# Fused Flamingo layer pair on one core: 7 of 32 low parts of the attention probabilities moved to VectorE, the casts of five batches' rows moved to ScalarE, three buffers of fp32 probabilities

## The reference, cut to what matters

```
def _L0_xattn_ref(X, encoder_output, causal_mask, padding_mask, Wq, bq, Wk, bk, Wv, bv, Wo, bo):
    ...
    scores = jnp.einsum('bgrqd,bgkd->bgrqk', q, k) / jnp.sqrt(jnp.float32(HD))
    scores = jnp.where(causal_mask[None, None, None, :, :], -jnp.inf, scores)
    scores = jnp.where(padding_mask[:, None, None, None, :], -jnp.inf, scores)
    w = jax.nn.softmax(scores, axis=-1)
    out = jnp.einsum('bgrqk,bgkd->bgrqd', w, v)
    out = out.reshape(b, H, LQ, HD).transpose(0, 2, 1, 3).reshape(b, LQ, HID)
    return out @ Wo.T + bo
x = x + jnp.tanh(g_xattn[0]) * _L0_xattn_ref(_layernorm(x, axis=-1), ctx_2048, mask_SxS2_bc0, mask_BxS2_bk0, ...)
```

## Time and profile before

| what | value |
|---|---|
| median of three executions | 1724.37 us (1722.57 to 1724.7) |
| span of the profiled execution | 1722.0 us |
| mean granted TensorE clock | 0.978 |
| phase A's 256 steps | 77 to 504 us of the span |
| busy over the whole span | PE 92%, DVE 57%, POOL 48%, ACT 41% |

### The profile page before, as it was taken

How to read it: one execution, slowest core, us unless ns; L and a number is a source line. 1 busy time by engine, 2 the same in 40 slices (tenths; PEclk the granted TensorE clock), 3 DMA queues, 4 the chain that set the end, 5 groups by cost and what they waited for, 6 DMA issues and landing times. The chain is left out here.

```text
span 1722.0 us, 29300 instructions
## 1 busy us (share of the span) xinstructions
PE 1587.8 (92%) x10826; PEld 829.3 (48%) x10826; DVE 973.1 (57%) x1947; ACT 709.2 (41%) x1311; POOL 824.3 (48%) x853
## 2 busy tenths in 40 slices
PE   5769999999877999899999989999999999999998
PEld 3336665665443444345656544444444444444443
DVE  5736666778736999845665543377454333211146
ACT  3268888888855655532232321211111111222221
POOL 3478887877853545443452434344333532112134
PEclk9989999999878999999999999999999999999999
DMA  6745444322333555444554426447454754477746
GB/s 182 160 102 112 99 106 109 93 67 72 92 73 84 110 119 114 93 86 86 96 120 95 78 74 156 110 105 153 92 101 101 154 101 95 109 173 172 168 138 195
DMA packets 453955, 195.68 MB, mean 114 GB/s; under 512 B 395500, under 2 KB 418286, under 8 KB 453816
## 3 DMA queue, kind: packets, MB, share of 16 engines
q1 hardware_dynamic: 448136, 175.19, 46.0%
q0 software_dynamic: 5680, 18.62, 4.1%
HBM read 77.17 MB, written 22.81 MB: 58 GB/s over the span
## 5 line engine op out<-in xcount | busy, mean ns | idle before, releaser
L1109 POOL TENSOR_TENSOR a_pl<-a_prob,a_ph 128x512 f16<-128x512 f32 x256 | 295.2, 1166 | 72.7 <-ACT a_prob L996 72.3
L1199 DVE TENSOR_REDUCE a_mx<-bank 128x2 f32<-128x512 f32 x256 | 173.3, 686 | 97.1 <-PE bank L690 95.5
L140 PE MATMUL bank<-XTh,d_whs 128*128 128x512 f16 x512 | 194.9, 381 | 4.2 <-PEq L89 2.4
L141 PE MATMUL bank<-XTl,d_whs 128*128 128x512 f16 x512 | 194.7, 380 | 0.0
L142 PE MATMUL bank<-XTh,d_wls 128*128 128x512 f16 x512 | 194.6, 380 | 0.0
L995 ACT ACTIVATE a_ph<-bank 128x512 f16<-128x512 f32 x256 | 153.9, 601 | 73.3 <-PE bank L710 35.9
L2384 POOL CAST d_cut<-d_raw 128x512 f16<-128x512 f32 x90 | 56.2, 624 | 227.7 <-DMA d_raw<-in_L_ffn_sw 146.8
L996 ACT ACTIVATE a_prob<-bank 128x512 f32<-128x512 f32 x256 | 154.4, 603 | 0.0
L2304 DVE TENSOR_TENSOR d_hid<-d_hid,bank 128x512 f32<-128x512 f32 x64 | 43.9, 686 | 172.1 <-PE bank L142 168.2
L2295 ACT ACTIVATE d_hid<-bank 128x512 f32<-128x512 f32 x64 | 38.2, 597 | 204.7 <-PE bank L142 204.7
L2299 ACT ACTIVATE d_hh<-d_hid 128x512 f16<-128x512 f32 x64 | 40.3, 630 | 194.7 <-DVE d_hid L2304 194.7
(11 more groups left out here) (349 smaller groups left out, 3996.4 us busy)
## 6 DMA issues: line engine op xcount, KB each, us to landing
d_raw<-in_L_ffn_w SPq DMA_DIRECT2D x48, 256.0 KB, 3.1
d_raw<-in_L_ffn_sw SPq DMA_DIRECT2D x42, 256.0 KB, 3.1
made<-e_y SPq DMA_DIRECT2D x39, 256.0 KB
a_stage<-in_L_ffn_w_fc SPq DMA_DIRECT2D x32, 256.0 KB, 2.9
a_stage<-in_L_ffn_w_proj SPq DMA_DIRECT2D x32, 256.0 KB, 3.1
a_fbuf<-in_ctx SPq DMA_DIRECT2D x16, 256.0 KB, 3.5
rows<-f_cut SPq DMA_DIRECT2D x16, 256.0 KB, 2.5
out_x<-X SPq DMA_DIRECT2D x16, 256.0 KB, 2.4
```

Of the source, the lines that this page charges most:

```text
L140: nc.tensor.matmul(out_ap, lhi, rhi, start=first, stop=False)
L141: nc.tensor.matmul(out_ap, lhi, rlo, start=False, stop=False)
L1109: nc.gpsimd.tensor_tensor(pl[:, n % NP, :], prob[:, n % 2, :], ph[:, n % NP, :], ALU.subtract).then_inc(ev["L"], 1)
L1199: nc.vector.tensor_reduce(mx[:, h, tt, half, 2 * (g % 4):2 * (g % 4) + 2], bank[BS + m % 2][:, :].rearrange("p (r k) -> p r k", r=2), AX_X ...
```

## The change

Three things are changed in phase A.

1. The low parts of steps n = 3, 8, 12, 15, 20, 22 and 27 of every batch (`BY_DVE`) are made by VectorE, in `low_part`, two steps later in its order: at the head of steps 5, 10, 14, 17, 22, 24 and 29. GpSimd skips them. There are two counters now, `L` and `LD`, and `low_done` chooses which one is waited for.
2. The casts of batches 3 to 7's context and x rows are made by ScalarE, at the end of steps 4 and 7 (context) and 15 and 18 (x), with the waits that went with them: for the load of the rows, for the earlier transposes, and for the writes of the context's parts to HBM. GpSimd keeps the subtractions, in steps 6, 9, 17 and 20.
3. `a_prob` has three buffers, and exponential n waits for low part n-3 in place of n-2.

```
-    NP = 4
-    prob = sb("a_prob", [P, 2, D])
+    NP, NR = 4, 3
+    prob = sb("a_prob", [P, NR, D])
...
+    BY_DVE = (3, 8, 12, 15, 20, 22, 27)
+
+    def low_done(eng, m):
+
+        b, n = m // NS, m % NS
+        if n in BY_DVE:
+            eng.wait_ge(ev["LD"], len(BY_DVE) * b + BY_DVE.index(n) + 1)
+        else:
+            eng.wait_ge(ev["L"], (NS - len(BY_DVE)) * b + n + 1 - sum(i < n for i in BY_DVE))
...
-                wait("L", b, n + 3, NS)
+                low_done(pe, b * NS + n)
...
+            def ctx_high(f, t):
+                act.wait_ge(c_in[t], 16 * f + 16)
+                act.wait_ge(x_tp[(f - 1) % 2], xt_count(f - 1))
+                nc.scalar.activation(fcut[:, t, 0, :], fbuf[:, t, :], ACT.Copy).then_inc(c_hi, 1)
+
+            def x_high(f, t):
+                act.wait_ge(n_nrm, 2 * f + t + 1)
+                act.wait_ge(c_tp[f % 2], ct_count(f))
+                act.wait_ge(c_wr, 64 * (f + 1))
+                nc.scalar.activation(fcut[:, t, 0, :], fbuf[:, t, :], ACT.Copy).then_inc(x_hi, 1)
...
-                    wait("L", b, n + 1, NS)
+                    if b * NS + n >= NR:
+                        low_done(act, b * NS + n - NR)
                     nc.scalar.activation(ph[:, n % NP, :], bank[BST + n % 2][:, :], ACT.Exp)
-                    nc.scalar.activation(prob[:, n % 2, :], bank[BST + n % 2][:, :], ACT.Exp).then_inc(ev["E"], 1)
+                    nc.scalar.activation(prob[:, (b * NS + n) % NR, :], bank[BST + n % 2][:, :], ACT.Exp).then_inc(ev["E"], 1)
...
+                    if b + 3 < B and n in (4, 7):
+                        ctx_high(b + 3, (n - 4) // 3)
...
+                    if b + 3 < B and n in (15, 18):
+                        x_high(b + 3, (n - 15) // 3)
...
-            FRONT = {2: (ctx_high, 0), 4: (ctx_low, 0), 7: (ctx_high, 1), 9: (ctx_low, 1),
-                     14: (x_high, 0), 16: (x_low, 0), 19: (x_high, 1), 21: (x_low, 1)}
+            FRONT = {6: (ctx_low, 0), 9: (ctx_low, 1), 17: (x_low, 0), 20: (x_low, 1)}
...
-                    pool.wait_ge(ev["E"], b * NS + n + 3)
...
+                    if n not in BY_DVE:
+                        pool.wait_ge(ev["E"], b * NS + n + 3)
...
+            def low_part(b, n):
+                wait("E", b, n + 3, NS)
+                nc.vector.tensor_tensor(pl[:, n % NP, :], prob[:, (b * NS + n) % NR, :], ph[:, n % NP, :],
+                                        ALU.subtract).then_inc(ev["LD"], 1)
...
                 for n in range(NS):
+                    if n - 2 in BY_DVE:
+                        low_part(b, n - 2)
```

More of the change, by code:

```diff
@@ L383, in phase_a @@
              "lk0", "lk1", "hv0", "hv1", "lv0", "lv1", "tq", "tq0", "tq1", "tk", "cq", "ck", "S", "M", "nm",
-             "nt", "nc", "ng0", "ng1", "ST", "E", "L", "AV", "ON", "To0", "To1", "hO0", "hO1", "lO0", "lO1", "O0", "O1", "x0", "x1", "ch")
+             "nt", "nc", "ng0", "ng1", "ST", "E", "L", "LD", "AV", "ON", "To0", "To1", "hO0", "hO1", "lO0", "lO1", "O0", "O1", "x0", "x1", "ch")
     ev = {n: sem("a_" + n) for n in names}
@@ L1024, in _ @@
         def _(pool):
-            pool.sem_inc(ev["L"], 2)
             nc.gpsimd.memset(mhalf[:, :], -0.5).then_inc(n_half, 1)
@@ L1101, in _ @@
                 x_low(2, t)
-            FRONT = {2: (ctx_high, 0), 4: (ctx_low, 0), 7: (ctx_high, 1), 9: (ctx_low, 1),
-                     14: (x_high, 0), 16: (x_low, 0), 19: (x_high, 1), 21: (x_low, 1)}
+            FRONT = {6: (ctx_low, 0), 9: (ctx_low, 1), 17: (x_low, 0), 20: (x_low, 1)}
             def body(b, par, more, more2):
                 for n in range(NS):
-                    pool.wait_ge(ev["E"], b * NS + n + 3)
-                    nc.gpsimd.tensor_tensor(pl[:, n % NP, :], prob[:, n % 2, :], ph[:, n % NP, :],
-                                            ALU.subtract).then_inc(ev["L"], 1)
+                    if n not in BY_DVE:
+                        pool.wait_ge(ev["E"], b * NS + n + 3)
+                        nc.gpsimd.tensor_tensor(pl[:, n % NP, :], prob[:, (b * NS + n) % NR, :], ph[:, n % NP, :],
+                                                ALU.subtract).then_inc(ev["L"], 1)
                     g, k = front_at(b, n)
```

## The result

The changed kernel takes 1733.84 us in the median of 5 runs (1730.85 to 1737.51), against 1724.37 before (1722.40 to 1727.35 with the runs beside it). The ratio is 1.0050, 95% interval 1.0037 to 1.0063: slower by 0.5%. The forecast was 1726.7, the range 1715 to 1736. The profiled execution of the changed kernel is the slowest of the five, 1737.51 us with a span of 1735.8: 3.7 above its median, and 13.8 us longer in span than that of before. So the two profiles lie 4.3 us further apart than the medians.

The account below looks back on a forecast made before the run. TensorE was taken to bound batches 1 to 5, nobody being full in 0, 6 and 7. Terms +7.3 (batches 1 to 5), -3.0, 0 and -2.0 gave +2.3 on 1724.4: 1726.7 us, range 1715 to 1736.

Parts of the forecast that it names:

- The frame: Batches 1 to 5: TensorE is in front, so a faster GpSimd gives almost nothing and any TensorE wait is paid in full.
- the rival in which the blocking decides: VectorE's subtractions always lose to GpSimd's at step 3, overrun at 8, 12, 15, delay batch 6: some 1736; chance 0.15.
- Step 3: `times_v(3)` waits for VectorE's low part, half a lost race with GpSimd counted: +1.1 us a batch in batches 1 to 4, +4.4.
- Step 20: `times_v(20)` waits for VectorE's low part behind v's: +1.1 us in batches 1 to 3, half in 4 and 5; +4.4.
- Steps 8, 12, 15: VectorE's low parts there fit into 1.77 us of room even when blocked, by 0.2; costed at nothing.
- Exponentials: TensorE's wait for exponentials, 0.3 us in batch 2, can go, 5 times: -1.5 us.
- Batch 0: Cast on ScalarE directly before exponential 5, -1.2 us, and quicker catching up behind the stall, -1.8: -3.0, ends 0 and -7.
- Batch 6: VectorE rises to 48.0 of 50.60 us and replaces GpSimd as the bound: 0, ends -3 and +5.
- Batch 7: No maxima, VectorE has room, ScalarE has 5.4 us idle and TensorE is not full: -2.0 us, ends 0 and -4.
- ScalarE's waits for GpSimd below 5 us: Sign that the forecast is right: ScalarE's waits for GpSimd in phase A, 34.2 us for low parts before, fall below 5.
- that the relief wins: Rival: with fewer GpSimd operations all runs earlier and batches 0, 6 and 7 gain: -10 us, 1714; chance 0.25.
- A late ScalarE: Rival: the context-write waits and the casts moved to ScalarE reach the exponentials: +6 us on top, 1733; chance 0.07.

Follow-up runs that it names:

- casts and buffers: The changed kernel with no low part on VectorE; casts on ScalarE and three buffers stay: 1719.76 us, ratio 0.9972 to the kernel before.
- the version without steps 3 and 20: The changed kernel with the low parts of steps 3 and 20 on GpSimd again, five of 32 on VectorE: 1714.7 us, ratio 0.9949.
- a remade one: The kernel with short low parts, where VectorE also computes step 3's low part once more beforehand into a spare tile: 1739.32 us, ratio 1.0072.
- the kernel with short low parts: The changed kernel with GpSimd's low parts of steps 5, 9, 13 and 23 cut to 16 of 512 columns: 1723.81 us, ratio 0.9996.
- three buffers alone: The kernel before with only the third buffer of fp32 probabilities: 1723.32 us, ratio 0.9986.
- the low parts alone: The changed kernel with the casts back on GpSimd; seven low parts on VectorE and three buffers stay: 1739.14 us, ratio 1.0088.
- the kernel before with the earlier load: The kernel before, with SyncE's load of batch 3's context rows issued ahead of the output weight's eight transposes: 1717.23 us, ratio 0.9963.
- the version one step earlier: The changed kernel with all seven VectorE low parts made at the head of step n+1 rather than n+2: 1721.96 us, ratio 0.9994.

## Why the prediction came out as it did

Slower was the likeliest of the three verdicts, and the time is within the stated range of 1715 to 1736. The frame held too: in batches 1 to 5 TensorE is in front, and there a relieved GpSimd gives little (3.0 us for casts and buffers, 257.6 us against 260.6). But the sum itself was off: +2.3 forecast, +9.5 measured in the medians and +13.8 between the profiles. 1733.8 lies just outside the forecast's own range of 1721 to 1733, and the range held it thanks to the rival in which the blocking decides. That the verdict came out is in part luck, for the sum's own 1726.7 lies below the 1727.8 from which slower was counted. Step by step, against the profile:

- **Step 3, forecast +1.1 a batch in batches 1 to 4: right as a net, and by luck.** I had counted half a lost race. VectorE lost it in all four, for which the forecast had 1.7. But a blocked low part costs 1.50 us, not 1.85, since GpSimd starts 0.2 us earlier; the pause is 1.80. Against that stands the wait of 0.7 for a maximum, which is gone. Net 1.1: two errors that cancel. The casts give that 0.7 also without any low part on VectorE: against the version without steps 3 and 20 the full 1.80 is lost.
- **Step 20, forecast +4.4: 3.5** (three times 0.94, twice 0.33). The place and the cause, v's low part directly in front, are as told.
- **Steps 8, 12, 15 at nothing: right.** In batch 2 those of steps 8 and 12 were blocked and took 1.52 and 1.53 us, and step 8's left 0.34; that of step 15 was free (0.68). TensorE waited for none of them in batches 1 to 5.
- **Exponentials -1.5: right in kind**; batch 2 has no such wait left.
- **The term that was missing: TensorE's clock.** Four stretches at half clock in batches 1 to 4, 6.8 us. I priced a pause at its own length. This is the step that failed: with 7.3 forecast and 15.4 measured for batches 1 to 5, 6.8 of the 8.1 missing are this. The idle time of TensorE there grew by 8.2, near the forecast: 10.9 of waits for VectorE's low parts and 1.8 for the turned maxima's transfer at the end of batch 1, less 4.7 of waits for maxima, exponentials and an output's low part that are gone. Several of the variants have the transfer's wait at that place, and what sets it stays open. The kernels with a short pause (no stretch) and with a remade one (two) show that stretches come with the pause of step 3; in the changed kernel two of the four did, 3.4 us, and the other two stood behind other waits.
- **What the clock is in the medians stays open.** The whole program's granted clock was 0.978 in the profile before, near the top of the 67 timed executions of that kernel (0.967 to 0.979, mean 0.973), and 0.972 in the profile of the change, at the bottom of its five (0.972 to 0.976, mean 0.974). So the two profiles differ more in their clock than the kernels do on average, and how much of the 7.2 us by which the median exceeds the forecast is the clock's isn't shown. What the timed executions do show is the same direction in the kernel with short low parts: 0.977 in the mean of twelve, where the changed kernel has 0.974.
- **Batch 0, forecast -3.0: measured -3.0**, again as a sum of two: TensorE's stall fell from 12.2 to 8.8 us, the catching up went quicker, and 4.2 us of new waits for VectorE's low parts took part of it back.
- **Batch 6, forecast 0: +1.5.** VectorE at 47.92 of 52.20 us is the bound, with four waits for its low parts, 3.3 us. **Batch 7, forecast -2.0: -1.8.**
- **ScalarE's waits for GpSimd below 5 us: gone altogether**; not one for a low part of GpSimd's is left. Its new wait for the context's writes, 4.3 us before on GpSimd, is 3.2, and TensorE waits for no exponential in batches 1 to 5.
- **Of the other signs**, batch 2's window grew by 3.3 us where 1 to 2 was written, and the wait at `times_v(3)` is 1.80 where about 1 was; that at `times_v(20)` is as told in batches 1 to 3.

Of the rivals, that the relief wins is refuted for the change as a whole, though the version without steps 3 and 20 reached its 1714; three buffers alone gain 1.2 us, casts and buffers 4.9. A late ScalarE is refuted too. That the blocking decides was half right: its first term, the race of step 3 always lost, is what happened, its second, an overrun at steps 8, 12 and 15, is not. Its threshold (a delay over 1.1 us) was not reached in batches 1 to 5, where the delay is 0.8 to 0.9. Still, taking the blocking away gives back 10 us: 3.3 are waits, since at step 3 the 0.8 lengthened the pause from 1.0 to 1.8, and with the longer pause came stretches at half clock. That step 3 and step 20 together cost 19.1 us by the medians, and apart 15.5 and 8.0, is measured and not explained.

## What to carry to other kernels

Work moved from a slower engine to a faster one is priced by where it lands in that engine's order, not by its duration: the same 0.68 us was free at five steps of batches 1 to 5, and cost 5 to 8 us in all at step 20 and 12 to 15 at step 3. Where TensorE is the bound, price a pause in its stream at more than its length (here up to 1.7 us more, behind about half of the pauses of 1.58 us and over), and look at the granted clock in the windows behind it. And read a long wait back to the queue that issued the transfer before giving work away: here one load, moved ahead of eight transposes, gained 7.8 us with nothing given away.

## What the runs showed of the hardware

**The clock after a pause.** In batches 1 to 5 of the fourteen profiled kernels the granted clock fell 16 times. In 15 cases TensorE had gone back to work 0.1 to 1.5 us earlier after a pause of 1.37 us or more; once, with the low parts alone, the pause was still going on. Of 23 pauses of 1.58 us and more, 10 were so followed, and in an eleventh the clock fell before its end; of 15 between 1.37 and 1.54 us 5 were, of 83 between 1.01 and 1.28 us none. The same pause of 1.80 us in the changed kernel's four batches was followed twice by a fall and twice not, and the wait of 1.54 us for `a_sums` was followed by one, at 292.8, in the kernel before with the earlier load, and not in the kernel before. So falls came only with pauses of 1.37 us and more, but such a pause doesn't by itself decide that one comes. The level is 0.50 (1.2 GHz), for 3.4 us each, once for 6.8. The Trainium skill, page TensorE: Matmul & The Clock Gate, section "Part 1: The HAM clock gate", says that activity releases the full clock and its absence takes it back, and that the same kernel meets this at different places from run to run. The traces agree with both: each of the 16 falls came with a pause, and equal pauses differ in what follows them.

**A two-column operation is held up like a large one.** In the kernel with the low parts alone VectorE's 128x2 operation at 200.40 takes 1.05 us beside a low part of GpSimd's, 0.17 in the kernel with short low parts. GpSimd's 128x2 operation at 202.49 takes 1.13 beside VectorE's low part and ends 0.54 after it. In the kernel with short low parts it starts first, at 149.61, takes 0.69, and VectorE's low part from 149.65 still takes no more than 0.70: it holds nobody up.

**Runs of the same instructions.** Ahead of phase A's steps before and after are the same, yet from 60 to 77 us the one profile has its clock at 1.00 and the other at 0.70:

```profile
60.00:77.00 17.00, 10.48 (x72) 1.00 0.54 134
...
60.00:77.00 17.00, 11.57 (x57) 0.70 0.43 86
```

Over the fourteen profiles the steps begin between 76.8 and 80.6 us, and what follows phase A, the same code in each, lasts 1214.7 to 1222.6 us. The record has the mean granted clock of every timed execution, and longer ones tend to have a lower one: of the twelve executions of the version one step earlier the fastest, 1718.78 us, had 0.979 and the slowest, 1730.97 us, 0.971. Differences of 2 to 4 us between medians of six runs are therefore not to be read as the work of an edit; the length of the part that was edited says more.
